# Unread matmuls on the identity in the prologue of a transformer-block kernel, ahead of the coefficients, the transpositions and the first projections

## What is computed

```python
gamma = (t @ gamma_w.T)[:, None, :]
beta = (t @ beta_w.T)[:, None, :]
n = gamma * (x * rsqrt(mean(x * x) + 1e-6)) + beta
q = split(n @ W_q.T); k = split(n @ W_k.T); v = split(n @ W_v.T)    # 16 heads of 16
attn = softmax(scale * einsum('bnqd,bnkd->bnqk', q, k))
x = x + a_alpha * (einsum('bnqk,bnkd->bnqd', attn, v) @ W_o.T)
# then n2 = conditioned norm of x, x = x + f_alpha * (silu(n2 @ gate) * (n2 @ hidden) @ out + out_b)
# then the layer norm with a tanh bias
```

## Time and profile before

| | |
|---|---|
| time, median of 3 runs | 821.73 us (821.41 to 822.71) |
| the profiled execution's own time | 823.76 us |
| its span, first to last instruction | 821.8 us |
| mean granted TensorE clock | 0.958 of 2.4 GHz |
| busy: PE, DVE, ACT, POOL | 734.0, 531.9, 469.8, 401.1 us |

### The profile page before, as it was taken

One profiled execution on the slowest core, in us unless ns is written; L12 is line 12 of the kernel. 1 busy time (PEld: TensorE's weight loads), 2 busy tenths in 40 slices (PEclk: granted clock), 3 DMA queues, 4 the chain that ended last, 5 costly groups with the idle time before them and its releaser, 6 DMA issues.

```text
span 821.8 us, 17472 instructions
## 1 busy us (share of the span) xinstructions
PE 734.0 (89%) x6646; PEld 496.0 (60%) x6646; DVE 531.9 (65%) x789; ACT 469.8 (57%) x854; POOL 401.1 (49%) x501
## 2 busy tenths in 40 slices
PE   4777879789998999899999999899989999998886
PEld 3423233445676667666676667666766667677785
DVE  3566467567766676768667776677767776345555
ACT  3346466567656666567665666566655665742331
POOL 3244232145338563666248462656356544763833
PEclk9769698999999999999999999999999999999998
DMA  6755465437441654335442644236333530221110
GB/s 183 255 195 172 139 201 163 155 90 216 132 148 54 214 138 166 106 105 198 127 156 59 243 144 155 66 132 193 118 130 106 187 99 14 81 82 51 47 47 26
DMA packets 63499, 108.74 MB, mean 132 GB/s; under 512 B 10192, under 2 KB 17800, under 8 KB 63416
## 3 DMA queue, kind: packets, MB, share of 16 engines
q1 hardware_dynamic: 62744, 106.91, 41.2%
q10 hardware_dynamic: 544, 0.52, 0.2%
q0 software_dynamic: 128, 0.20, 0.1%
HBM read 59.60 MB, written 39.09 MB: 120 GB/s over the span
## 4 chain that ended last, share of the span: by engine, by line
PE 69%; DVE 9%; DMA 7%; issue 5%; ACT 4%; POOL 3%; SPq 2%; POOLq 0%; ACTq 0%; DVEq 0%
PE ps_x L1254 15%; PE ps_o L1227 12%; PE ps_j L1144 11%; PE ps_j L1267 9%; PE ps_s L1214 9%; PE ps_m L1199 6%; DVE mx L970 3%; DMA qs<-m_hl 2%; PE ps_o L1267 2%; ACT prob L803 2%; DMA stack_scratch<-qk_lo 2%; DMA n_x<-n 1%; PE ps_m L1254 1%; PE ps_s L1254 1%; DVE fx L952 1%
## 5 line engine op out<-in xcount | busy, mean ns | idle before, releaser
L970 DVE TENSOR_REDUCE mx<-ps_m 128x2 f32<-128x1024 f32 x222 | 271.6, 1223 | 140.6 <-PE ps_m L1199 140.1
L803 ACT ACTIVATE prob<-ps_s 128x1024 f32<-128x1024 f32 x256 | 261.7, 1022 | 98.0 <-PE ps_s L1214 97.3
L1214 PE MATMUL ps_s<-qs,ks 64*128 64x512 f32 x512 | 124.0, 480 | 30.9 <-ACT prob L803 16.1
L1214 PEld LDWEIGHTS ps_s<-qs,ks 64*128 64x128 f32 x512 | 49.7, 190 | 156.3 <-issue 83.4
L1227 PE MATMUL ps_o<-prob,v 128*32 128x512 f32 x1024 | 143.1, 632 | 0.0
L565 POOL TENSOR_TENSOR xr<-xr,sc 128x512 f32<-128x512 f32 x43 | 56.0, 1303 | 110.3 <-DVE sc L982 59.6
L1199 PE MATMUL ps_m<-ks,qs 64*128 64x512 f32 x444 | 94.7, 422 | 10.9 <-DVE mx L970 8.0
L540 POOL TENSOR_TENSOR a_lo<-act_y,a_hi 128x256 fp32r<-128x256 f32 x100 | 73.4, 734 | 54.9 <-ACT a_hi L834 54.7
L1254 PE MATMUL ps_x<-n,gh_hi 64*128 64x256 f32 x872 | 98.7, 286 | 1.6 <-DVE act_y L1017 1.6
L1254 PE MATMUL ps_x<-n_x,gh_hi 64*128 64x256 f32 x872 | 94.8, 277 | 2.2 <-DMA n_x<-n 2.2
L1254 PEld LDWEIGHTS ps_x<-n,gh_hi 64*128 64x128 f32 x872 | 75.7, 188 | 12.1 <-DVE act_y L1017 8.0
(11 more groups left out here) (175 smaller groups left out, 1447.5 us busy)
## 6 DMA issues: line engine op xcount, KB each, us to landing
qs<-stack_scratch SPq DMA_DIRECT2D x32, 512.0 KB, 4.1
ks<-stack_scratch SPq DMA_DIRECT2D x32, 512.0 KB, 5.0
stack_scratch<-qk_hi SPq DMA_DIRECT2D x56, 256.0 KB, 2.9
out_scratch<-o_raw SPq DMA_DIRECT2D x32, 256.0 KB, 2.2
n_x<-n SPq DMA_DIRECT2D x32, 256.0 KB, 3.7
stack_scratch<-qk_lo SPq DMA_DIRECT2D x28, 256.0 KB, 3.2
xa<-in_x SPq DMA_DIRECT2D x8, 512.0 KB, 4.2
on_lo<-out_scratch SPq DMA_DIRECT2D x16, 256.0 KB
```

The costliest lines, as they stand in the source:

```text
L803: act.activation(prob[:, n % 2, 2 * h:2 * h + 2, :], ps_s[:], ACT.Exp, scale=SCALE).then_inc(p_r, 1)
L970: dve.tensor_reduce(mx[:, group % 2, :, h, qt], max_pair(mp)[:], AX.X, ALU.max).then_inc(mx_red, 1)
L1214: mm = pe.matmul(ps_s[:, s, :], ks[r:r + 64, g, j, kb * P:(kb + 1) * P], qs[r:r + 64, g, j, :], start=True, stop=True)
```

## The change

A helper `warm_up(times)` issues that many matmuls with the identity both as weights and as moving operand, into the first 128 columns of `ps_m`, where nobody reads them. Five stand ahead of the coefficients, four between coefficients and transpositions, nine between transpositions and projections. The wait for the identity moves to the very front, and the nine wait for the first `n_hi`.

```diff
+            def warm_up(times):
+
+                for _ in range(times):
+                    pe.matmul(ps_m[:, 0, 0:P], ident[:], ident[:], start=True, stop=True)
+
+            pe.wait_ge(consts, 6)
+            warm_up(5)
             pe.wait_ge(small_in, 16 * 3)
             coefficients(0, ps_o)
-            pe.wait_ge(consts, 6)
+            warm_up(4)
             transposes(0, 0, ps_j)
             transposes(0, 1, ps_g)
+            pe.wait_ge(n_hi_r, 1)
+            warm_up(9)
             pe.wait_ge(w_lo_r, 1)
             for q, bank in enumerate((ps_s[:, 0], ps_s[:, 1], ps_m[:, 0], ps_m[:, 1])):
                 project_qk(0, q, bank)
```

## The result

| | before | changed |
|---|---|---|
| median | 822.5 us (19 runs) | 825.93 us (19 runs) |
| lowest to highest | 820.21 to 825.92 us | 822.02 to 830.14 us |
| ratio, 95% interval | | 1.0036 (1.0020 to 1.0052) |
| profiled execution: own time, span, clock | 823.76, 821.8 us, 0.958 | 822.02, 820.1 us, 0.962 |

The forecast was 820.5 us, with a range of 819.4 to 822.9. The measured time is above the range, and the change is a loss of 3.4 us between the medians where a gain of 1.2 was forecast. The forecast also started from a median of three runs, 821.73 us, and that of 19 is 822.5. The profiled execution of the changed kernel happens to be the fastest of its 19 runs. Its whole span says nothing of the median, and it can be read only stage by stage.

The account below looks back on a forecast made before the run. The prologue was taken as one chain through twelve projection matmuls at the low clock. + 1.05 (late transpositions) - 2.34 (full clock) - 0.1 (tail) + 0.2 (bunched writes) = -1.2 us, from 821.73 to 820.5 us; range 819.4 to 822.9.

Parts of the forecast that it names:

- The fillers' price: On TensorE, each of a filler's two instructions takes 0.22 us at the low clock and 0.125 us at the full one.
- Rival 3: Load and stream don't overlap in a plain fp32 matmul, so fillers overrun: + 2.2 us, 823.9 us; chance 0.06.
- The five are covered: Ahead of the coefficients: ten instructions over at 8.15 us, the DMA comes at 8.26; cost 0, cover left 0.1 us.
- The four stand on the path: Ahead of the transpositions, no cover: they start 1.2 us late, and the chain stands 1.05 us late at ACT.
- The clock: TensorE's clock rises 6.2 us after the first filler, at 12.15 us, with two of four transpositions still slow.
- Rivals 1 and 2: Coefficients and transpositions don't keep the clock going, 821.6 to 822.7, chance 0.30; fillers count for nothing, 824.0, chance 0.06.
- The nine are covered: Ahead of the projections: over at 15.9 us, under n_lo's 16.5; cost 0 at the full clock, cover 0.6 us.
- The DMAs behind: Six writes and the read back after the projections: of 1.4 us gained, 1.2 pass; read back at 25.2, not 26.38.
- the prize of 2.34 us: Twelve projection matmuls on the chain take 2.78 us at the full clock instead of 5.12; at most 2.34 us gained.
- The whole shift passes ... The loop behind starts 1.2 us earlier.: From read back through reductions and row maxima nothing has a fixed hour, so the loop starts 1.2 us earlier.
- Rival 4: Clock is right, but the shift is lost in the DMAs behind or the loop: 821.2 to 822.2 us; chance 0.10.

Follow-up runs that it names:

- the lateness alone: Kernel before without fillers, transpositions waiting for five clearings of an unused tile on POOL; 823.88 us, 1.0025 against before.
- f1_five_2_nine: Changed kernel with two fillers in the place of the four, five and nine kept; 823.90 us, 1.0026 against the kernel before.

## Why the prediction was wrong, point by point

- *The fillers' price.* Taken at 0.22 and 0.125 us, measured 0.23 and about 0.12. Rival 3 (no overlap of load and stream) fell.
- *The five are covered.* Right, but barely: ten instructions end near 8.4 us. In twelve of the thirteen profiles with the five, the coefficients' weight load still waits for its DMA behind them. In f1_five_2_nine the DMA landed earlier and the load waits for the fillers. Five alone cost + 0.2, with an error of 0.6.
- *The four stand on the path.* Right in kind and size: 1.2 us forecast, 1.6 in the first profile, 1.9 in the mean of four (12.37 against 10.47 us in before's two), of which some 0.3 are a later DMA of the coefficients. The four alone (+ 1.9) and the lateness alone (+ 1.6) show that it passes to the end.
- *The clock.* I took the rise 6.2 us after the first filler; it was 7.3 us in the first profile (13.2). In the second both sets of transpositions still ran at the low clock (1.06 us each), and the rise came while the nine ran. The projections were at the full level in all four. Rivals 1 and 2 fell. The Trainium skill says (TensorE: Matmul & The Clock Gate, Part 4: PE-mode transpose) that the full clock does not engage for transpositions, which do not count as TensorE being busy in the same way. In the first profile the clock rose during them, right behind fillers, and four took 0.67 us against 1.06. They did not keep it from rising; whether they alone could raise it, no run shows.
- *The nine are covered.* Right in the changed kernel: in three of its profiles the projections wait for n_lo behind them, in the second they end with it. But where the clock rises only while they run, as in the nine alone and in five and nine, they hold the projections up by 0.3 to 0.8 us. The warm projections pay for that.
- *The DMAs behind: a step that failed.* "Of the 1.4 us, 1.0 to 1.4 pass; I take 1.2" took the landing of the last write as 2.9 us and nothing for the read back. Its own figures don't agree: it has the writes done at 25.5 us at the earliest and the read back at 25.2, and rows 2 had 3.19 us for that very write. The stages of the chain in the means of four profiles of the changed kernel and two of before, in us, show what came in its place:

  | | before | changed |
  |---|---|---|
  | first transposition at | 10.5 | 12.4 |
  | to the first projection | 4.9 | 4.9 |
  | to the issue of the last write | 7.5 | 5.5 |
  | to the first `max_scores` | 8.4 | 10.1 |
  | to the first scores | 16.9 | 16.8 |

  The warm projections win 2.0 us, and the write and the read back lose 1.7 of them. That isn't due to the four. From the issue of the last write to the first `max_scores` it takes 9.2 to 11.4 us in all 14 profiles in which the twelve projections are warm, and 8.3 to 9.5 in the other six. In the changed kernel the last write lands 4.46 to 4.74 us behind its issue, where nine other profiles with warm projections have 3.76 to 3.96, the one with two fillers 5.34, and before's two 3.19 and 3.37. In seven of the nine the read back of `ks` makes up for it, with 5.4 to 6.9 us instead of the changed kernel's 4.7 to 5.2. The first read back goes at 26.9 to 27.9 us in the changed kernel, where 25.2 was forecast.

  So the prize of 2.34 us was mostly gone before the first scores, whatever stood ahead of the transpositions: the nine alone win 0.5 us from the first projection to the first scores. That six writes issued closer together (within 3.1 us instead of 3.8) cause it is likely and not shown; with eight fillers they were issued within 3.6 us, and the last took 3.86. Nor is it the rate of the queue alone that sets the end: from 26 to 28 us, in the changed kernel's first profile, the DMA share is 0.03, and SP waits for the last write until 27.28.
- *"The whole shift passes ... The loop behind starts 1.2 us earlier."* This is the step that failed most. The first scores come 1.4 us later and not 1.2 earlier (49.7 us in the mean of four, against 48.2): 1.9 from the late transpositions, less the 0.4 that is left of the warm projections. And the sum ended at the first scores, and took the rest of the span as the same. It is not: of the + 4.2 us over all four measurements, about 1.4 lie ahead of the first scores, and 2.8 behind. The reading of rows 1 under it, that the clock is low in the first fifth only, was too short: the last slice there is an 8, and from 740 to 822 us before's clock is 0.93. Over the 20 profiles of all kernels, the rest of the span grows by 0.36 us for each us at the lower clock behind the first scores (correlation 0.85; 42.6 to 61.3 us of it, rest 769.6 to 777.8 us). Of the changed kernel's extra 6.4 us at the lower level, some 2 lie ahead of the first scores, where DVE and DMAs set the pace. The other 4.3 are worth 0.36 x 4.3 = 1.5 us by that line, or 1.3 by the 0.29 of the 367 runs. This part is a correlation, no experiment: no run changes the loop's clock and nothing else.
- *What stays open.* Some 1.3 to 1.5 us of the 4.2 are in no account. And no run shows why the loop loses the clock more often behind this prologue than behind one with the same lateness but without the four, although both issue the same work from the first scores on. The two differ in more than the four: the delay on POOL moves POOL's and DVE's work ahead of the transpositions too. The distance between those two, 2.6 us with an error of about 0.7, came out of both pairs of measurements; its place in the loop differs from profile to profile.
- *Rival 4* had named the loop's clock, at 821.2 to 822.2 us and a chance of 0.10, as something that could only eat the gain. That it could be a loss nearly twice as large as the prize was in none of the cases. Slower had 0.12.

No version beats before in both of its measurements. The nine alone are nearest, at 0.9967 and 0.9996.

## What to carry to other kernels

A filler that raises the clock is free only where it stands inside a wait that the trace shows. The five (2.3 us into a wait until 8.26) cost nothing that was measured; the nine (4.1 us at the low clock into a wait of 3) overran it and were paid back by warm projections; the four (1.9 us into one of 0.42) delayed everything behind them. Before counting on faster matmuls, look at what drains them. Here a write and a read back took 1.7 of the 2.0 us that TensorE had won. And where runs of one program spread by 1.2% (818.1 to 827.9 us for the kernel before), one profile is one draw: repeat the whole and each part, and compare the mean granted clocks of many runs, not two spans.

## What was not expected of the hardware

- The start of the coefficients, set by one DMA, moved between 7.95 and 9.29 us from execution to execution of kernels with the same DMAs ahead of it. A cover of 0.1 us, as I had counted for the five, is none.
- The granted clock falls and rises at other places in each profile of the same kernel. The time at the lower level behind the first scores was 44.0, 56.1, 61.0 and 61.3 us in four profiles of the changed kernel, with spans of 820.1, 826.4, 827.2 and 824.9 us.
- Four DVE instructions (`nx`, L1046) take 2.85 us in all three profiles in which POOL clears tiles beside them, and 1.81 in the changed kernel's.
